# Products of a constant tile into an unused bank at TensorE's waits, in a two-layer attention kernel

## The reference, cut to what matters

```
x = x + gated_attention(cond_attention_0(x))    # 16 heads of 64 with one shared key and value, a bias by
                                                # distance and a null key; then 16 heads of 16 columns, whose
                                                # 8 blocks of 64 keys are closed where the probability is small
x = x + feed_forward(experts_0(x))
x = x + chunked_attention(cond_attention_1(x))
x = x + routed(experts_1(x))

routed: weights = x @ router_w; the 63 rows of each sequence with the largest go through
  h = rmsnorm(x_sel); a = softmax(rope(h wq) rope(h wk)^T + mask); x1 = x_sel + (a h wv) wo
  x2 = x1 + gelu(rmsnorm(x1) w1) w2;  out[sel] = x2 * weights[sel]
```

## Time and profile before

| | us |
|---|---|
| median of 3 runs | 2753.78 (2753.34 to 2756.57) |
| profiled execution, its own time | 2752.22 |
| its span, first to last instruction | 2750.4 |
| TensorE busy in matrix products | 2598.3, 94% of the span |
| VectorE, ScalarE, GpSimd busy | 1432.5, 1057.8, 913.1 |
| mean granted clock of TensorE | 0.977 |

### The profile page before, as it was taken

The page is one execution under the profiler, slowest core; times in us unless marked ns, Lnnn a source line. Parts: engine busy times, 40 slices in busy tenths (PEclk is TensorE's granted clock), DMA queues, the critical chain, the costliest instruction groups (busy, mean ns, idle before and its releaser), DMA issues. The chain is left out here.

```text
span 2750.4 us, 36762 instructions
## 1 busy us (share of the span) xinstructions
PE 2598.3 (94%) x13249; PEld 1524.6 (55%) x13249; DVE 1432.5 (52%) x3215; ACT 1057.8 (38%) x2459; POOL 913.1 (33%) x953
## 2 busy tenths in 40 slices
PE   7999998889998899999999999999999899899998
PEld 4465655533333348748758658556555557544456
DVE  7466564466667344234243233555645577655545
ACT  4767675344544211111121111265656545311222
POOL 3656564177778122102103102465555210000000
PEclk9999999889999899999999999999999999999998
DMA  4000000000000330000000010233323100400000
GB/s 154 1 1 1 1 1 20 11 10 11 12 13 9 102 129 0 1 0 1 0 0 1 0 41 1 88 116 92 119 77 112 37 1 1 127 0 2 2 10 26
DMA packets 82619, 91.91 MB, mean 33 GB/s; under 512 B 14982, under 2 KB 66064, under 8 KB 82313
## 3 DMA queue, kind: packets, MB, share of 16 engines
q1 hardware_dynamic: 82120, 89.04, 10.4%
q0 software_dynamic: 320, 0.52, 0.1%
HBM read 83.19 MB, written 2.14 MB: 31 GB/s over the span
## 5 line engine op out<-in xcount | busy, mean ns | idle before, releaser
L1013 POOL TENSOR_TENSOR cb_sc<-cb_toep,cb_mk 128x128 f32<-128x128 f32 (+3 forms) x256 | 215.8, 871 | 194.5 <-ACT cb_pr L1051 183.4
L1013 POOL TENSOR_TENSOR cb_bias<-cb_bias,cb_mk 128x128 f32<-128x128 f32 (+3 forms) x256 | 215.2, 871 | 153.6 <-DMA cb_bias<-in_fside_16xSxS 153.3
L399 PE MATMUL PS<-ident,cb_pr 128*128 128x128 f32 x1280 | 195.6, 284 | 24.0 <-ACT cb_pr L1051 21.7
L1652 DVE TENSOR_REDUCE gb_bmax<-PS 128x16 f32<-128x1024 f32 x128 | 156.4, 1224 | 110.8 <-PE PS L1431 110.5
L399 PEld LDWEIGHTS PS<-ident,cb_pr 128*128 128x128 f32 x1280 | 135.9, 141 | 115.8 <-issue 104.8
L700 DVE CUSTOM_DVE_ANT_0 cb_sc<-PS,cb_sc,cb_sneg 128x128 f32<-128x128 f32 (+3 forms) x256 | 130.0, 548 | 125.5 <-PE PS L388 124.2
L3305 POOL TENSOR_TENSOR eb_S<-ff_h 128x1024 f32<-128x1024 f32 x16 | 38.0, 2376 | 465.7 <-PE PS L2225 465.6
L1431 PE MATMUL PS<-gb_ks,gb_qs 32*128 32x512 f32 x512 | 150.2, 675 | 33.6 <-DVE gb_bmax L1652 28.5
L1810 ACT ACTIVATE gb_pt<-PS 128x1024 f32<-128x1024 f32 x128 | 130.4, 1023 | 133.8 <-PE PS L1437 127.3
L700 DVE CUSTOM_DVE_ANT_0 cb_bias<-PS,cb_bias,cb_sneg 128x128 f32<-128x128 f32 (+3 forms) x256 | 129.4, 547 | 89.7 <-PE PS L388 88.8
L1058 ACT ACTIVATE cb_pt<-PS 128x128 f32<-128x128 f32 (+3 forms) x448 | 162.4, 409 | 34.8 <-PE PS L399 34.3
(11 more groups left out here) (557 smaller groups left out, 5052.1 us busy)
## 6 DMA issues: line engine op xcount, KB each, us to landing
cb_bias<-in_fside_16xSxS SPq DMA_DIRECT2D x64, 256.0 KB, 2.9
cb_bias<-in_fside_16xSxS SPq DMA_DIRECT2D x64, 192.0 KB, 2.5
ff_h<-in_L_ffn_h_w SPq DMA_DIRECT2D x2, 4096.0 KB, 23.0
cb_bias<-in_fside_16xSxS SPq DMA_DIRECT2D x64, 128.0 KB, 2.2
cb_toep<-rel_table SPq DMA_DIRECT2D x8, 512.0 KB, 7.5
cb_bias<-in_fside_16xSxS SPq DMA_DIRECT2D x64, 64.0 KB, 2.3
ff_w<-in_L_ffn_w_w SPq DMA_DIRECT2D x3, 1024.0 KB, 8.0
gb_ks<-ga_room SPq DMA_DIRECT2D x64, 32.0 KB, 2.0
```

The costliest lines, as they stand in the source:

```text
L399: ins = pe.transpose(PS[:, bank, j * P:j * P + P], pr[:, v % 2, e, j * P:j * P + P], ident)
L1013: ins = pool.tensor_tensor(biases(v, e), turned(h, n) if L0 else biases(v, e), mk[:, b % 2, packed(t):packed(t) + n], ALU.add)
L1652: dve.tensor_reduce(bmax[:, n % 2, t, g:g + 2, 0:NB], PS[:, bank:bank + 2, :].rearrange("p g (n k) -> p g n k", k=64), AX.X, ALU.max)\
```

## The change

A helper issues a given number of plain products with the identity tile as the stationary operand and a constant tile of 128 x 512 as the moving one, all into one bank that nobody reads, with no semaphore. In the text below such a product is called a filler. They are added at these places:

- conditioned attention, both layers: 2 before the last unit is turned, 1 before `values` of the last pair, 2 before the eight `spread`;
- gated attention: 1 before the loop; 2 ahead of the scores of each unit i = 1 to 7 of period n = 0 (14 in all); in period 16 one ahead of each unit i = 4 to 7; in period 17 one ahead of i = 3 and of i = 6;
- last rows: 1 before `mix_values`, 2 before `turn_mixed`, 1 each before `token_out`, `turn_normed`, `hidden` and `processed` of sequence 3 (7 in all).

The one new wait (`ca_D` at N - 1) stands ahead of the fillers at the last unit and lets them write bank 0 only when VectorE has read the scores of unit N - 2 from it.

```diff
+def keep_busy(pe, out, ident, x, count):
+
+    for _ in range(count):
+        pe.matmul(out, ident, x, start=True, stop=True)
...
+            def idle_work(count):
+                keep_busy(pe, PS[:, 0, :], ident, w["wq"][:, 0, 0:S], count)
...
                     values(*divmod(v // NT - 1, MC))
+                if v == N - 1:
+                    pe.wait_ge(sm["ca_D"], N - 1)
+                    idle_work(2)
                 turn(v)
...
+            idle_work(1)
             values(B - 1, MC - 1)
             turn_rows(("rd", B - 1), 2 * B if L0 else B)
             turn_null(B - 1)
+            idle_work(2)
             for m in range(MC):
                 spread(("rb", B - 1, m), m, ("rd", B - 1))
...
             own_gates(0)
+            keep_busy(pe, PS[:, 6, :], ident, hTs[:, 0, :], 1)
             for n in range(-1, GROUPS + 2):
                 for i in range(UNITS):
+                    if n == 0 and i:
+                        keep_busy(pe, PS[:, 6, :], ident, hTs[:, 0, :], 2)
+                    elif n == GROUPS and i >= 4 or n > GROUPS and i in (3, 6):
+                        keep_busy(pe, PS[:, 0, :], ident, hTs[:, 0, :], 1)
...
+                def idle_work(count):
+                    keep_busy(pe, PS[:, 0, :], ident, wr["w1"][:, 0, 0:S], count)
...
                     turn_choice(3)
+                    idle_work(1)
                     mix_values(late, 3)
+                    idle_work(2)
                     turn_mixed(late, 3)
+                    idle_work(1)
                     token_out(late, 3)
                     back_to_rows(late, 2)
+                    idle_work(1)
                     turn_normed(late, 3, 1)
+                    idle_work(1)
                     hidden(late, 3)
+                    idle_work(1)
                     processed(late, 3)
```

## The result

The changed kernel takes 2743.34 us, median of 5 runs (2741.34 to 2745.28), against 2753.78 before: a ratio of 0.9954, with a 95% interval from 0.9940 to 0.9969. It is faster, by 10.4 us where 15.8 were forecast. The profiled execution took 2743.42 us, with a mean granted clock of 0.988 in place of 0.977.

What follows compares the result with a forecast made beforehand. TensorE was taken as the bound, its clock halved in 17 stretches (122.10 us) after short waits. Terms 2.9 + 1.4 + 0.4 + 0 + 4.6 + 0.9 + 5.2 = 15.4 us gave 2738 us, range 2730 to 2748.

Steps and rivals of the forecast that it cites:

- the price of a filler: All edited places: one 128x512 product costs 0.47 us at full clock, 0.94 at half, nothing inside a longer wait.
- Period 0: Second gated period: fillers add 1.7 us, the half-clock stretch from 542.10 us gives back 1.7; sum nothing.
- Period 1: Gated period after the filled one: 4.6 us won, middle of 2.3 (fall two steps later) and 6.9 (full clock).
- The last rows: Final chain of steps: 5.2 us won, middle of 7.4 if the clock holds and 3.0 if it falls in `mix_values`.
- The attentions' ends: Ends of first and second conditioned attention: 2.9 and 1.4 us won by full clock, fillers costing nothing inside waits.
- Before the loop: One filler in the 13.60 us half-clock stretch before the gated loop: 0.4 us won, between -0.9 and 1.7.
- The gated end: End of gated attention: stretch from 924.40 us gives 1.4 back, one uncovered filler costs 0.47; net 0.9 us won.
- A: Rival: clock holds through period 1 and last rows, stretch before the loop is cut; 21.2 us won, 2733; chance 0.18.
- B: Rival: falls only move, to early period 1 and `mix_values`, gated end gives nothing; 9.1 us won, 2745; chance 0.25.
- C: Rival: clock held at the attentions' ends alone; 4.3 us won, 8.1 lost, 2758; chance 0.07.
- D: Rival: slower, fillers don't hold the clock and stand before TensorE's own work; 8.1 us lost, 2762; chance 0.05.
- The price of a halved clock: Skill page's rule, half the throttled time: 28.9 us over six stretches, less 3.2 for uncovered fillers, time 2728.

Runs made afterwards that it cites:

- the ends alone: Kernel before with only the fillers at the ends of the two conditioned attentions, all others taken out: 2756.08 us, ratio 1.0001 (0.9988 to 1.0015).

## Why the prediction was right, and where it was off

The time lies in the range (2730 to 2748), faster as said, 5.3 us above the forecast of 2738. The mechanism was the forecast's: with fillers the clock stays at full where it fell, and period 1 and the last rows are won by fillers that stand ahead of them.

**The step that failed is the price of a filler**, "four such products in 1.88 us at full clock", "so I price one at 0.47 us". The x4 of the earlier trace rows counts records, and a plain float32 product leaves two, so the row shows two products. The sections ahead of the prediction, and the prediction itself, count records as products elsewhere too: by the source `mix_values` and `hidden` are 16 products each, not 32, `processed` and the last `values` 8, not 16. Not every product leaves two: the eight turned tiles are x8, and so are the eight `spread`, whose operands the kernel declares as float32r. Three of these start 0.235 us apart in the changed kernel's trace (476.215, 476.450, 476.685), with 512 columns each. The right reading is 0.94 us for one, and 0.86 for each further one in a row, by the doubled count. Every cover was compared with half the true length. At half clock it is twice as much; the one before the loop took 2.08 us, not 0.94. By this the mechanism stands and the term was mis-sized by half.

**Period 0** was given a cost of 1.7 us. With pairs of 1.72 us the covers leave 1.0 at unit 1, 0.4 at units 2, 4, 6 and 7, 1.7 at unit 3 and 1.4 at unit 5, in sum 5.7; less the 1.7 of the stretch at 542, which did go, makes 4.0, and 4.4 was measured. The forecast had it at nothing: this is the largest error. Unit by unit, the starts are later by 0.9 us at unit 1, 0.5 at units 2, 4, 6 and 7, 1.4 at unit 5 and 0.1 at unit 3, where the stretch at 542 went. So one sign that the prediction had named for being wrong did show, a step of line 1431 over 3.4 us: the step to unit 5 takes 3.88. Half the width, which has the price that the forecast assumed, measured -0.2 against the forecast's 0.

**Period 1** was put at 4.6, the middle between a fall that comes later (2.3) and none (6.9). It was 6.7 in this trace and 4.1 to 6.7 over the nine kernels with fillers in period 0, 5.5 in the mean. The doubt was real: six of the nine had a short stretch there.

**The last rows** were put at 5.2 and gave 4.4, by two errors that offset each other. The clock held through `mix_values` in all nine, which the forecast doubted; and the seven fillers cost 3.3 us bare, not 1.0 (0.86 twice where there is no cover, 0.84, 0.40, 0.20 and 0.09 elsewhere). The gain ahead of that cost is then 7.7 us, where 8.4 had been added up. Narrow fillers, at half the price, lie bare for 0.9 us by the same working and give 6.8, which makes 7.7 again.

**The attentions' ends** were 2.9 and 1.4, measured 2.5 and 1.1: the pair ahead of `spread` is longer than its wait. With narrow ones they were 2.8 and 1.4. But the first of these falls happens in two of five profiled executions without fillers, so its term should have been weighted; a filler pays there on some runs, and on the others the wide pair costs some 0.3 us. That is one reason why the ends alone did not show in the time.

**Before the loop** the forecast was 0.4 won, with bounds of 0.9 lost and 1.7 won. It was 1.0 here and 0.4 to 3.8 over the nine kernels with this filler, 2.2 in the mean, against 0 to 0.4 in the four experiments without it (by the starts, up to 530 us). The term was too small, and its upper bound too: the short stretch at 525 goes in eight of the nine, and in some executions half of the long one too. **The gated end** was put at 0.9 won. With the start of the experts it was 1.2 won, but not for the reason given: the stretch at 924 went, one of 6.8 us came at 892.5, ahead of the first filler at 914, and the one behind 936.9 is 6.8 us long, not 13.6. Kernels without these fillers lie between 3.5 us longer and 4.5 shorter there, those with them between 3.4 longer and 1.7 shorter. In twelve of the thirteen traces, with these fillers and without, 3.1 to 3.3 us are lost between 670 and 905 us, ahead of them, and behind 905 both kinds have cases with nothing won and with over 4 us won. Whether they help at all stays open.

**The rivals.** A had the clock right in period 1 and in the last rows and the cost wrong. B (2745) is nearest in time but not in cause: the falls of the edited parts did not move into `mix_values` or period 1 of this trace. C is excluded by the same rows, and D, since the clock was held; the 0.94 us that it put on a filler for half clock is the true price at full clock. What the prediction did not see at all is the +5.4 us elsewhere: new stretches in unedited code. The repeat of the same program with 9.7 us more says that such stretches come and go from one execution to the next, so one profiled execution doesn't show that its unedited parts are an effect of the change. It doesn't exclude one either: between the second attention's end and the last rows the eight traces with the whole change or a variant of it are 2.9 to 14.1 us longer than the first trace of the kernel before, the five others 0.0 to 4.7. No run settles that.

**Luck.** The edited parts gave 12.5 us in the trace where 15.4 were added up. Period 0 fell short by 4.4, the last rows by 0.8 and the ends by 0.7; period 1 gave 2.1 more than the middle that was taken for it, the part before the loop 0.6 and the gated end 0.3. So part of the nearness is luck: a price at half its true size was in part made good by middles that came out low. Two slips of the prediction change nothing: B's sum has 0.4 won at the gated end where its own words leave 0.47 lost, which would make it 2746, and a further stretch at half clock, from 2747.1 to the end with no product in it, stands beside the 17 that it counts.

**The price of a halved clock.** Two stretches of 20.45 us were taken away; the work in them became 6.7 and, by the estimate above, 7.7 us shorter, 14.4 of 40.9. By the Trainium skill, "TensorE: Matmul & The Clock Gate", section Terms, it would be half, 20.5. The trace disagrees with that: the waits for VectorE and ScalarE in such a stretch do not shorten (a unit's wait in the trace before is 1.33 us at 541.50, at full clock, and again at 566.66, at half), so here the rule gives an upper bound. The Trainium skill, "TensorE: Matmul & The Clock Gate", section Back-to-back issue gap, gives N / 2.4 + 2.5 ns at full clock for a single product of N columns, an estimate of 216 ns at 512. A record of a filler here follows the last by 430 ns, and there are two, so this rule would price a float32 filler at a quarter of what was measured; the 235 ns of the float32r `spread` above is near it. No run tried fillers of that type.

## What to carry to other kernels

Before a row of the timeline is used as a price, find out what its count counts: here the known number of instructions in the source against the x of the row would have shown two records to a float32 product. Size work that only fills a wait by the shortest wait it stands in: with 256 columns in place of 512 the clock was held as well in period 0, at the ends and in the last rows, and most of the cost was gone (2736.5 us against 2746.3 for the wide ones, with the six fillers of periods 16 and 17 out as well). And profile the kernel before more than once when the gain is a fall of the clock that doesn't happen: here one stretch came in five of five executions, and another in two of five, which can't be counted in full.

## What the runs showed of the hardware that was not expected

- A plain float32 product with 512 moving columns and a full stationary tile shows as two records and occupies TensorE for 0.86 us at full clock when others stand in front of it; with 256 columns a pair takes 1.03 to 1.13 us with its lead-in, with 128 0.61 to 0.71. A float32r product with 512 columns shows as one record, and the next one starts 0.235 us later.
- Fourteen small products (seven pairs of 0.61 to 0.71 us, one in front of each unit) kept the clock at 1.00 through period 0 where TensorE still waited 0.69 us a unit.
- The same program had its falls of the clock at different places in different executions: the changed kernel was profiled at 2743.4 and at 2753.1 us, the kernel before at 2752.2 and at 2761.5.
